# 64 small products in two halves, and a new set of due times, in a gated delta rule on one core

## The reference, cut to what matters

```python
M = jnp.where(tri_s, jnp.einsum('bhnci,bhndi->bhncd', k_b, k) * decay, 0.0)
Tinv = jax.scipy.linalg.solve_triangular(eye + M, eye, lower=True)
u = Tinv @ v_b
w = Tinv @ (k_b * jnp.exp(g)[..., None])
attn_loc = jnp.where(tri, jnp.einsum('bhnci,bhndi->bhncd', q, k) * decay, 0.0)
...
v_new = u_i - w_i @ S
o_i = qg_i @ S + a_i @ v_new
S = S * jnp.exp(gl_i)[..., None, None] + jnp.einsum('bhck,bhcv->bhkv', kd_i, v_new)
```

## Time and profile before

| what | value |
|---|---|
| runs | 1562.03, 1567.06, 1572.85 us |
| median | 1567.06 us |
| profiled execution, its own time | 1574.62 us |
| its span | 1572.9 us |
| mean granted clock of TensorE | 0.944 |
| PE / PEld / DVE / ACT / POOL busy | 90 / 67 / 66 / 54 / 34% |

### The profile page before, as it was taken

How to read it: one execution, slowest core, us unless ns; L and a number is a source line. 1 busy time by engine, 2 the same in 40 slices (tenths; PEclk the granted TensorE clock), 3 DMA queues, 4 the chain that set the end, 5 groups by cost and what they waited for, 6 DMA issues and landing times. The chain is left out here.

```text
span 1572.9 us, 35680 instructions
## 1 busy us (share of the span) xinstructions
PE 1421.1 (90%) x13996; PEld 1060.8 (67%) x13996; DVE 1044.4 (66%) x2150; ACT 855.3 (54%) x1728; POOL 532.1 (34%) x562
## 2 busy tenths in 40 slices
PE   4569999998989999999999999999899976998998
PEld 3335767777777767777777777777678764555855
DVE  6977684876758685776858587786745534674344
ACT  4345665655556665656556665656445316576210
POOL 3841332341423333242323234233326436541100
...
GB/s 171 45 36 44 26 35 16 52 42 12 32 9 45 23 52 29 25 31 10 45 9 63 31 25 27 15 45 17 27 97 54 28 102 0 1 1 28 55 9 19
DMA packets 142485, 56.39 MB, mean 36 GB/s; under 512 B 109776, under 2 KB 134992, under 8 KB 142064
## 3 DMA queue, kind: packets, MB, share of 16 engines
...
HBM read 37.11 MB, written 16.97 MB: 34 GB/s over the span
## 5 line engine op out<-in xcount | busy, mean ns | idle before, releaser
L1147 POOL TENSOR_TENSOR og<-og,sz 128x256 f32<-128x256 f32 x128 | 93.0, 727 | 576.4 <-DVE og L1090 354.8
L684 PE MATMUL banks<-wz,xT 128*128 128x256 f32 x512 | 132.7, 404 | 14.1 <-DVE yacc L1110 14.1
L937 DVE SCALAR_TENSOR_TENSOR Yv<-banks,cwall,Yv 128x511 f32<-128x511 f32 (+2 forms) x192 | 129.3, 741 | 11.5 <-ACT Yv L777 11.4
L755 PE MATMUL banks<-wo,oT 128*128 128x256 f32 x512 | 127.7, 395 | 0.3 <-ACT oT L929 0.3
L540 PE MATMUL banks<-wqk,xT 128*128 128x512 f32 x256 | 126.2, 620 | 0.3 <-DVE Yk L937 0.2
L540 PE MATMUL banks<-wv,xT 128*128 128x512 f32 x256 | 121.1, 618 | 5.0 <-DVE Yv L937 5.0
L684 PEld LDWEIGHTS banks<-wz,xT 128*128 128x128 f32 x512 | 96.5, 198 | 38.2 <-issue 25.2
L755 PEld LDWEIGHTS banks<-wo,oT 128*128 128x128 f32 x512 | 98.3, 202 | 13.4 <-ACT oT L929 0.8
L924 ACT ACTIVATE junk<-og 128x512 f32<-128x512 f32 x64 | 40.4, 630 | 121.0 <-POOL og L1147 120.9
L1154 POOL TENSOR_TENSOR rn<-ss,c_half 128x4 f32<-128x4 f32 x64 | 64.5, 1007 | 100.2 <-DVE ss L1104 100.1
L1110 DVE TENSOR_TENSOR yacc<-yacc,banks 128x512 f32<-128x512 f32 x64 | 43.8, 685 | 71.8 <-PE banks L755 70.8
...
## 6 DMA issues: line engine op xcount, KB each, us to landing
...
blk<-cm_d SPq DMA_DIRECT2D x128, 16.0 KB, 1.8
...
Td<-t_d SPq DMA_DIRECT2D x128, 16.0 KB, 1.9
```

Of the source, the lines that this page charges most:

```text
L684: ins = pe.matmul(bank[7][:, b * 256:(b + 1) * 256], xT[:, d, b * S + q, :], wz[:, d, :], start=(d == 0), stop=(d == KD - 1))
L755: ins = pe.matmul(bank[7][:, b * D:(b + 1) * D], oT[:, b, h, :], wo[k % 2][:, h, :], start=(h == 0), stop=(h == VR - 1))
L937: v.scalar_tensor_tensor(y, bank[b][:, 0:T - j], conv_w(k, t)[:, 3 - j:4 - j], y, ALU.mult, ALU.add).then_inc(s["tap"].sem, 1)
L1147: pool.tensor_tensor(og[:, n, :, :], og[:, n, :, :], sz[q % 2][:, b, :].rearrange("p (h d) -> p h d", h=VR), ALU.mult).then_inc(s["osz"].s ...
```

## The change

`pe_blocks` now takes the part of the 16 blocks that it issues and gives back its last instruction. P16 and TU16 are each issued as blocks 0 to 7 and, after a `yield` of a due time of its own (P16x, TU16x), blocks 8 to 15; the waits stay ahead of the first half and the signal behind the second. All four tables are replaced, and so are TURN and FSTEP.

```diff
--- before.py
+++ after.py
@@ -329,56 +329,56 @@
-TURN = 69.77
-FSTEP = 7.25
+TURN = 69.95
+FSTEP = 7.34
...
 AT = {
-    "g": 16.97, "wqk": 38.48, "wv": 105.06, "cm": 145.49, "base": 121.05, "wz": 147.68, "E0": -30.41, "E1": -84.4, "E2": -87.54, "E3": -132.69, "exp0": -30.19, "exp1": -105.86,
-    "exp2": -78.22, "exp3": -206.38, "pk0": -5.11, "pk1": -2.84, "pk2": -161.19, "pk3": -155.41, "k0": 4.77, "k1": 11.28, "k2": -115.16, "k3": -239.33, "ks": 15.89, "kT0": 16.69,
-    "kT1": -195.1, "kt0": -100.78, "kt1": -35.36, "nk": 16.36, "KK0": 21.35, "KK1": -160.1, "nE0": 11.82, "nE1": -119.87, "nrm": -60.07, "CM0": 22.34, "CM1": -40.04, "pq0": 14.72,
-    "pq1": 17.69, "pq2": -132.6, "pq3": -269.97, "q0": 17.13, "q1": 17.02, "q2": -211.91, "q3": -173.58, "qs": 28.36, "qT0": 26.99, "qT1": -58.44, "sq0": -24.57, "sq1": -107.93, "nq": 35.59,
-    "QK0": -83.18, "QK1": 19.62, "AT0": -113.85, "AT1": -357.87, "pv0": 23.6, "pv1": -503.2, "pv2": -341.96, "pv3": -329.48, "v0": 28.13, "v1": 29.95, "v2": -237.26, "v3": -327.38,
-    "vs": 36.56, "pw0": 34.89, "pw1": -83.96, "pw2": -128.56, "pw3": -250.94, "w0": -19.65, "w1": 46.53, "w2": 52.38, "w3": 42.17, "ws": 50.4, "vT0": 52.25, "vT1": 7.09, "vT2": 54.51,
-    "vT3": -78.42, "vn0": 53.37, "vn1": -210.76, "vn2": 59.12, "vn3": -79.14, "sub0": 39.57, "sub1": -16.86, "sub2": 14.94, "sub3": -121.17, "zero": 20.77, "U0": 58.31, "P16": 51.59,
-    "P16c": 56.14, "TU16": 55.26, "T16": 60.64, "U16": -9.1, "UBd": -7.75, "Tf": 59.55, "P32": 60.44, "P32c": -70.39, "TU32": 64.33, "T32": 72.73, "U32": 75.49, "P64a": 72.12, "PU64": 77.95,
-    "P64ac": -236.8, "P64bc": 80.11, "U64b": 81.88, "U64ac": 62.82, "U64bc": 81.58, "zp0": 3.72, "zp1": -318.46, "z": 7.02, "KS": -189.9, "R": -252.74, "QS": 4.6, "TR": 4.79, "V": 6.36,
-    "V2": -219.19, "AV": 7.89, "SU": -227.29, "S": 14.04, "og": 7.93, "Sd": -180.66, "osz": 3.57, "ssq": 1.14, "red": 3.19, "rn": -7.27, "ogn": -615.51, "oTp": 7.24, "oT": 9.45,
-    "wout0": 12.53, "wout1": -60.52, "y": 18.23, "RECUR": 91.86, "STEP": 8.71, "OUT": 19.89,
+    "g": -11.53, "wqk": -25.18, "wv": 62.7, "cm": 81.53, "base": 10.72, "wz": 122.2, "E0": -32.3, "E1": -184.36, "E2": -164.92, "E3": -80.8, "exp0": -29.88, "exp1": -147.81, "exp2": -87.43,
+    "exp3": -229.65, "pk0": -5.37, "pk1": -0.7, "pk2": -196.38, "pk3": -262.96, "k0": 8.91, "k1": 11.4, "k2": -91.6, "k3": -178.72, "ks": 15.06, "kT0": 13.99, "kT1": -219.23, "kt0": -104.77,
+    "kt1": -75.07, "nk": 17.08, "KK0": 21.66, "KK1": -139.6, "nE0": 14.1, "nE1": -123.96, "nrm": -202.29, "CM0": 22.53, "CM1": -1.81, "pq0": 13.79, "pq1": 17.8, "pq2": -11.85,
+    "pq3": -279.74, "q0": 17.41, "q1": 21.45, "q2": -187.56, "q3": -180.99, "qs": 28.83, "qT0": 28.09, "qT1": 1.42, "sq0": -2.6, "sq1": -190.44, "nq": 31.87, "QK0": -8.67, "QK1": -48.02,
+    "AT0": -24.62, "AT1": -464.83, "pv0": 22.34, "pv1": -471.52, "pv2": -415.81, "pv3": -270.42, "v0": 28.05, "v1": 28.63, "v2": -120.62, "v3": -222.07, "vs": 34.88, "pw0": 33.77,
+    "pw1": -80.19, "pw2": -92.81, "pw3": -221.75, "w0": 19.49, "w1": 48.45, "w2": -33.27, "w3": 49.57, "ws": 50.39, "vT0": 51.94, "vT1": -20.89, "vT2": 56.38, "vT3": -32.94, "vn0": 53.01,
+    "vn1": -17.6, "vn2": 57.08, "vn3": -24.89, "sub0": 39.13, "sub1": -129.15, "sub2": -20.89, "sub3": -185.15, "zero": 12.91, "U0": 55.26, "P16": 51.9, "P16x": -94.04, "P16c": 51.1,
+    "TU16": 56.44, "TU16x": -49.81, "T16": 58.41, "U16": -124.39, "UBd": -9.08, "Tf": 60.93, "P32": 58.88, "P32c": -110.25, "TU32": 61.75, "T32": 70.86, "U32": 70.67, "P64a": 71.71,
+    "PU64": 77.63, "P64ac": -143.56, "P64bc": 80.89, "U64b": 82.58, "U64ac": 82.92, "U64bc": 38.24, "zp0": 2.5, "zp1": -312.43, "z": 6.92, "KS": -286.17, "R": -253.71, "QS": 6.06,
+    "TR": 4.04, "V": 6.16, "V2": -160.62, "AV": 7.45, "SU": -165.95, "S": 11.2, "og": 8.07, "Sd": -122.51, "osz": 11.27, "ssq": 1.59, "red": 0.55, "rn": 3.33, "ogn": -595.74, "oTp": 7.59,
+    "oT": 9.25, "wout0": 12.25, "wout1": -122.52, "y": 14.95, "RECUR": 93.01, "STEP": 8.68, "OUT": 19.87,
 }
...
 FIRST = {
...
-    "P16": 54.85, "P16c": 62.83, "TU16": 63.65, "T16": -334.26, "U16": -278.95, "UBd": -213.82, "Tf": 73.78, "P32": -61.67, "P32c": -163.98, "TU32": -112.94, "T32": 32.88, "U32": 24.35,
+    "zero": 43.73, "U0": 57.43, "P16": 52.08, "P16x": 36.23, "P16c": 69.52, "TU16": 62.63, "TU16x": -49.48, "T16": -414.4, "U16": -336.93, "UBd": -342.02, "Tf": -47.91, "P32": -88.47,
...
 FINAL = {
...
-    "vn0": -373.1, "vn1": -168.21, "vn2": -322.85, "vn3": -415.1, "sub0": 33.37, "sub1": -385.89, "sub2": 40.12, "sub3": -104.13, "zero": 48.14, "U0": 56.83, "P16": 55.82, "P16c": 59.26,
-    "TU16": 63.28, "T16": 68.88, "U16": -104.27, "UBd": -17.4, "Tf": 64.67, "P32": 65.94, "P32c": -95.95, "TU32": 70.49, "T32": -513.76, "U32": 73.43, "P64a": -12.7, "PU64": 2.15,
+    "vT3": 43.08, "vn0": -196.68, "vn1": -334.24, "vn2": -396.85, "vn3": -466.01, "sub0": 34.21, "sub1": -445.72, "sub2": 39.83, "sub3": -132.75, "zero": -8.24, "U0": 60.38, "P16": 57.74,
+    "P16x": -9.6, "P16c": 59.44, "TU16": 61.95, "TU16x": 23.96, "T16": 74, "U16": -2.96, "UBd": -104.42, "Tf": 65.31, "P32": 66.68, "P32c": -238.98, "TU32": 70.55, "T32": -442.38,
...
 START = {
-    "x": -377.01, "iota": -129.92, "small": -168.8, "const": -121.77, "q1in": 358.1, "q1out": 104.62, "fill": -85.68, "fill2": 23.74, "q0r": -78.03, "q0p": -110.71, "tb": -410.13,
-    "px": -372.13, "prs": -617.81, "xn": -429.93, "xTp": -501.16, "xT": -47.11, "pba": 8.49, "abeta": -412.82, "ba": -200.06, "asp": -45.59, "sp1": -96.25, "asp2": -213.92, "sp2": 2.3,
-    "pgs": -85.41, "gc": -428.06, "pgT": -114.15, "gp": -118.15, "atab": -450.88, "neg": -44.19, "g_d": 15.49, "qin": -365.41, "qin2": -133.23, "qc": -47.61, "qr": -4.28, "qp": -2.76,
-    "qt": 21.39, "qe": 32.43, "r1": 134.78, "q1s": 155.99, "q1t": 164.82, "q1c": 179.32, "q1p": 19.51, "q1tp": 179.06, "q1e": 510.3, "f0x0": -9.1, "f0x1": 74.61, "f0in": 155.96, "f0": 64.85,
-    "f0y": 348.04, "fill1": 113.91, "cwp": -293.69, "cwe": -25.83,
+    "x": -504.12, "iota": -143.49, "small": -296.22, "const": -332.62, "q1in": 347.52, "q1out": -52.61, "fill": -33.02, "fill2": 22.79, "q0r": -143.2, "q0p": -103.48, "tb": -396.66,
+    "px": -317.07, "prs": -604.22, "xn": -417.83, "xTp": -389.68, "xT": -121.92, "pba": 8.49, "abeta": -348.05, "ba": -186.23, "asp": -85.74, "sp1": -100.8, "asp2": -341.81, "sp2": 5.5,
+    "pgs": -206.48, "gc": -499.97, "pgT": -201.66, "gp": -152.55, "atab": -280.91, "neg": -28.22, "g_d": -171.11, "qin": -306.61, "qin2": -172.12, "qc": -107.67, "qr": -1.16, "qp": -1.66,
+    "qt": 19.49, "qe": 34.12, "r1": 136.07, "q1s": 160.43, "q1t": 159.84, "q1c": 179.5, "q1p": 19.51, "q1tp": 181.87, "q1e": 429.03, "f0x0": 49.7, "f0x1": 108.09, "f0in": 142.99,
+    "f0": 65.41, "f0y": 434.88, "fill1": 114.72, "cwp": -266.98, "cwe": -30.81,
 }
...
@@ -589,11 +589,11 @@
                 ins = pe.transpose(bank[q % 2][:, (2 * b + h) * P:(2 * b + h + 1) * P], Yv[:, h, b, q * P:(q + 1) * P], c["ident"][:, :])
         ins.then_inc(s["vTp"].sem, 1)
 
-    def pe_blocks(pe, name, out, lhs, rhs):
-        for i in range(HC):
+    def pe_blocks(pe, part, out, lhs, rhs):
+        for i in part:
             for g in quarters:
                 ins = pe.matmul(out[g, i * C:(i + 1) * C], lhs(g, i), rhs[g, i, :], start=True, stop=True)
-        ins.then_inc(s[name].sem, 1)
+        return ins
 
     def pe_decays(pe, k):
         for r in range(4):
@@ -622,11 +622,15 @@
         yield at(k)["P16"]
         pe.wait_ge(*s["base"](7, k))
         pe.wait_ge(*(s["Eexp"](3, k + 1) if k + 1 < HK else s["AT"](1, k)))
-        pe_blocks(pe, "P16p", b2, lambda g, i: CMf[g, i, g], Td)
+        pe_blocks(pe, range(HC // 2), b2, lambda g, i: CMf[g, i, g], Td)
+        yield at(k)["P16x"]
+        pe_blocks(pe, range(HC // 2, HC), b2, lambda g, i: CMf[g, i, g], Td).then_inc(s["P16p"].sem, 1)
         yield at(k)["TU16"]
         pe.wait_ge(*s["P16"](0, k))
         pe.wait_ge(*s["U0"](0, k))
-        pe_blocks(pe, "T16p", b3, lambda g, i: Ud[g, i, :], P2)
+        pe_blocks(pe, range(HC // 2), b3, lambda g, i: Ud[g, i, :], P2)
+        yield at(k)["TU16x"]
+        pe_blocks(pe, range(HC // 2, HC), b3, lambda g, i: Ud[g, i, :], P2).then_inc(s["T16p"].sem, 1)
         yield at(k)["P32"]
         pe.wait_ge(*s["T16"](0, k))
         for i in range(HC):
```

2 lines of the change are left out of this document (added), and 36 rows, old and new, of tables (FINAL, FIRST).

## The result

The changed kernel took 1572.3 us at the median of 20 runs (1559.9 to 1581.0), the kernel before, on the same chip, 1566.5 us (1558.3 to 1582.8). The ratio is 1.0042, with a 95% interval from 1.0023 to 1.0060: by this ratio 6.6 us slower (the medians differ by 5.8). That is within the 1% that I had called no change, and within my range, but on the other side of the kernel before than the 1564 us of the forecast. The profiled execution of the changed kernel is a long one, 1581.0 us with a span of 1579.1, so its stretches are compared with those of before and not its total.

A forecast was written before the change was run, and what follows sets the result against it. TensorE's own instruction list was taken to bound the kernel, leaving only short waits to win. Middle -7.0, start +4.4 and last head -0.6 gave 1567.1 - 3.2 = 1564 us on the median, range 1551 to 1580.

The forecast's parts named there:

- The halves: P16 and TU16 sets on TensorE: both halves stand side by side in all 16 heads, same 128 instructions, cost 0.
- The start: xT ahead of ScalarE's first cast: gate chain +2.6 us, one comparison +1.2, P16c +0.6; sum +4.4, bounds 0 and +8.
- step 3: Middle heads, TensorE: the decays go ahead of AV[1], SU[1], KS[2]; same products fill the same time, so 0.
- step 2: Middle heads: kT ahead of oTp[2], so key's norm, CM and blocks come earlier; gain 0.3 us a head, bounds 0 and 0.72.
- 4 us each: Sign for step 2: VectorE's wait for blk and TensorE's for yacc each smaller by this in total.
- more breaks in the first set: Rival, slower: Td sooner removes waits, so all 14 heads' first sets break off; 1588 us, chance 0.09.
- step 1: Middle heads: P64a ahead of wout[1], T32 wait goes; gain 0.2 us a head, bounds 0.39 gain and 0.3 loss.
- The whole middle: Fourteen heads at 0.2 + 0.3 us gain: -7.0 us, bounds -15.5 and +4.2.
- The last head: Keys' scores and CM before the query's taps, saving part of the zp wait: -0.6 us, between -2 and +2.
- The break in the first set: TensorE stands 1.79 us after 102 of 128 instructions; seven heads break, such a head taking 3.4 us more.

The follow-up runs named there:

- joined: Changed kernel's order of every engine's list, with the two sets of 64 products issued whole; 1.0056 (1.0031 to 1.0081) of the kernel before.
- newstart1: Kernel before, with the changed kernel's order only up to head 0's first block inverse; 1.0072 (1.0040 to 1.0104) of the kernel before.
- quiet: As gate, but GpSimd's first ternary group put off behind the gate chain and its two memsets moved ahead; 0.9992 of the kernel before.
- gate: Kernel before, with only ScalarE's order at the very start changed (xT before first cast, three casts before the gate steps); 1.0041 of the kernel before.
- mid_kT: Kernel before, with only TensorE's query product, kT0 and kT1 ahead of oTp[2] in heads 1 to 12; 1.0038 of the kernel before.
- hop: Kernel before, with one more SyncE transfer ahead of the load of Td in each head, so Td alone comes later; 1.0146 of the kernel before.

## Why the prediction was wrong

The size was small either way; the sign was wrong because the term of the start was mis-sized, at +4.4 for a measured +11. Two steps of the middle were priced wrongly too, but there the errors nearly cancel.

*The halves: 0.* Right, by the timeline and by joined.

*The start: +4.4, bounds 0 to +8. Measured +11 (11.0 and 11.3 by two pairs of runs; newstart1's interval is 6 to 16).* This is the term that turned the result, and it lies outside my bounds, though its interval reaches into them. The cause that I named was right and its size as well: cwall 2.4 us later, for 2.6. What I had left out is that work moved on one engine's list meets other work. GpSimd's operation now runs beside the gate chain, and those of the group that moves ahead of the inverse beside head 0's inverse, and each holds a VectorE operation until it ends: 3.1 us more than before in the gate chain, 6.8 us in the four products (7.7 us instead of the 0.9 of before). I had priced the comparison that moves ahead at its own 1.21 us alone. My rows of the start show ScalarE and VectorE and no line of GpSimd, so what ran beside the gate chain was not in my sum; the kernel before already had L241 at 1.38 us there.

The traces show the hold at each place: in the changed kernel the four held products, of two inputs (1.99, 1.76, 2.02 and 1.96 us), end within 0.13 us of the end of the GpSimd TENSOR_TENSOR beside them, the one beside a memset isn't held (0.21 us, as in the kernel before), and quiet takes the hold of three operations away with GpSimd's work alone (L238 1.78 us in gate and 0.42 in quiet, L241 1.23 and 0.29, L1277 1.74 and 0.17). Why some operations are held and others are not no run shows. Had I counted the holds, the +4.4 would have become up to 4.4 + 3.1 + 6.8 = 14.3, if all of it reached TensorE; measured are 11, and the first set of head 0 is 10.6 us later.

*Middle, step 3 (decays ahead of AV[1]): 0. Measured -8 by itself.* I had written that the same products fill the same time. They don't quite: zp waits for yacc 5.2 us in all instead of 9.0 in the window, and TensorE comes to the first set ahead of Td in 10 heads instead of 4. All waits together (issue, Td, yacc) shrink by 2 of the 8 us; the granted clock of the window rises from 0.97 to 0.99, and that the rest comes from there is argued, not shown.

*Middle, step 2 (kT ahead): -4.2. Measured +6 by itself, nothing with the decays.* In the changed kernel VectorE's wait for the blocks fell from 10.8 to 8.6 us and TensorE's for yacc from 14.1 to 9.3, where I had named 4 us each. But mid_kT shows that this is not the step's doing: there the blocks' wait is 11.8 us, and that for yacc 8.7 instead of 9.0 in the window. With nine breaks for seven it looks like the rival that I gave 0.09, "more breaks in the first set", but 4 to 8 breaks occur with the old middle too, so the cause of the 6 us stays open. In the changed kernel the decays' step hides it.

*Middle, step 1 (P64a ahead): -2.8.* The weight load no longer waits for Tf in most heads (2.2 us in 3 instead of 6.2 in 16), as named. What it is worth was not measured by itself. The whole middle is -5.8 (-9.6 to -1.9), my -7.0 within that; as two of its parts were wrong, the agreement is luck.

*The last head: -0.6.* The rest of the end is near that (-3.1, interval -7.8 to +1.4), and what the other terms leave for the whole end is 6.6 - 11 + 5.8 = +1.4. But I had missed that the decays of head 15 move the other way from all others, behind zp[1] of head 13. The wait of 3.1 us there is in the profile; its share of the 6.6 us is not settled (above).

*The break in the first set.* The prediction left its cause open. The traces put it beside the packets of the instruction queue: each of the 99 breaks of over 0.2 us ends 2.17 to 2.82 us after such a packet starts, in heads 2 to 13 at a place that goes with the head, and in hop a wait ahead of the set is deducted from it (four sets, wait and break together 1.6 to 2.0 us). From a head that breaks off to the next are 3 us more than from one that does not (70.4 against 67.2 and 67.5), against the 3.4 of the forecast.
